# The feed-forward part runs on inside the attention's programs: normalisation in the last phases, last tile in two parts, weights split in the first

## The reference, cut to what matters

```python
x = _layernorm(x + _L0_attn_ref(x, ...), axis=-1)
x = _layernorm(x + _L0_xattn_ref(x, ctx_1024, ...), axis=-1)
x = _layernorm(x + _L0_ffn_ref(x, ...), axis=-1)
...
# _L0_xattn_ref
q = rmsnorm(q, gq)
k = rmsnorm(k, gk)
scores = jnp.einsum('bqhd,bkhd->bhqk', q, k) * scale
attn = jax.nn.softmax(scores, axis=-1)
out = jnp.einsum('bhqk,bkhd->bqhd', attn, v)
return out @ Wo
...
# _L0_ffn_ref
h = jax.nn.gelu(jnp.einsum('lne,he->lnh', x, proj1) + proj1_bias, approximate=False)
out = jnp.einsum('lnh,eh->lne', h, proj2) + proj2_bias
```

## Time and profile before

| | |
|---|---|
| runs | 1362.12 us median, 1360.58 to 1363.41 |
| the profiled execution | 1365.66 us, of it the span 1363.8 us |
| TensorE, busy | 1321.3 us (97%), mean granted clock 0.984 |
| DVE, ACT, POOL, busy | 1104.1 us (81%), 1026.5 us (75%), 1040.8 us (76%) |
| DMA | 45.59 MB, 33 GB/s over the span |
| phase -1 (first key projections) | about 166 to 202 us |
| phase 16 | about 1259 to 1296 us |
| last block | 1296.5 us to the end |

### The profile page before, as it was taken

One profiled execution on the slowest core, in us unless ns is written; L12 is line 12 of the kernel. 1 busy time (PEld: TensorE's weight loads), 2 busy tenths in 40 slices (PEclk: granted clock), 3 DMA queues, 4 the chain that ended last, 5 costly groups with the idle time before them and its releaser, 6 DMA issues. The chain is left out here.

```text
span 1363.8 us, 25118 instructions
## 1 busy us (share of the span) xinstructions
PE 1321.3 (97%) x6366; PEld 1041.6 (76%) x6366; DVE 1104.1 (81%) x1742; ACT 1026.5 (75%) x3157; POOL 1040.8 (76%) x926
## 2 busy tenths in 40 slices
PE   8889899999999999999999999999999999999878
PEld 4667578777777777777777777777777777778667
DVE  5766589888888888888888888888888888875275
ACT  2557688888888888888888888888888888843342
POOL 3733212898989898989898989898989898998840
PEclk9799999999999999999999999999999999999979
DMA  7040000101010101010100000000000010010200
GB/s 246 32 166 1 25 1 9 38 12 35 13 35 13 36 12 34 12 35 12 34 15 32 16 30 19 29 20 26 24 23 27 19 31 16 18 68 25 71 0 28
DMA packets 28012, 45.59 MB, mean 33 GB/s; under 512 B 2720, under 2 KB 23840, under 8 KB 27120
## 3 DMA queue, kind: packets, MB, share of 16 engines
q1 hardware_dynamic: 27168, 44.25, 9.9%
q10 hardware_dynamic: 720, 0.10, 0.0%
HBM read 40.41 MB, written 3.93 MB: 33 GB/s over the span
## 5 line engine op out<-in xcount | busy, mean ns | idle before, releaser
L1302 PE MATMUL xa_k_ps<-wk_parts,xa_ctxT_hi 128*125 128x512 f32 x768 | 377.1, 491 | 6.1 <-DVE wk_parts L1295 5.0
L1245 DVE TENSOR_REDUCE xa_ss<-xa_sq 125x6 f32<-125x768 f32 x360 | 339.4, 943 | 1.0 <-ACT xa_sq L1183 1.0
L1233 DVE TENSOR_TENSOR xa_scores<-xa_s_ps,xa_rk 125x448 f32<-125x448 f32 x384 | 238.5, 621 | 99.8 <-PE xa_s_ps L1304 98.0
L1303 PE MATMUL xa_k_ps<-wk_parts,xa_ctxT_hi 128*125 128x512 f32 x768 | 304.1, 396 | 0.0
L1304 PE MATMUL xa_k_ps<-wk_parts,ctxT_lo 128*125 128x512 f32 x768 | 303.1, 395 | 0.0
L1095 POOL TENSOR_TENSOR xa_den<-probs,xa_den 125x896 f32<-125x896 f32 x128 | 272.2, 2126 | 0.0
L1168 ACT ACTIVATE probs<-xa_scores 125x896 f32<-125x896 f32 x192 | 183.6, 956 | 105.2 <-POOL xa_scores L1084 39.3
L1148 ACT ACTIVATE xa_sq<-xa_k_ps 125x512 f32<-125x512 f32 x360 | 212.2, 589 | 42.3 <-PE xa_k_ps L1304 21.8
L1182 ACT ACTIVATE xa_k_ps<-xa_k_ps 125x128 f32<-125x128 f32 x720 | 189.2, 263 | 30.7 <-PE xa_k_ps L1304 28.6
L1387 PE MATMUL xa_o_ps<-probs,xa_ctx_nat 125*128 125x448 f32 x448 | 205.4, 539 | 0.0
L1084 POOL TENSOR_TENSOR xa_scores<-xa_scores,xa_gmax 125x896 f32<-125x896 f32 x96 | 203.9, 2124 | 0.1
(11 more groups left out here) (186 smaller groups left out, 2364.7 us busy)
## 6 DMA issues: line engine op xcount, KB each, us to landing
xa_ctx_nat<-in_ctx SPq DMA_DIRECT2D x16, 750.0 KB
ctxT_in<-in_ctxT SPq DMA_DIRECT2D x84, 125.0 KB, 2.1
qo<-in_xq_w SPq DMA_DIRECT2D x1, 2048.0 KB, 11.0
qo<-in_xo_w SPq DMA_DIRECT2D x1, 2048.0 KB, 19.0
vo_scratch<-qo SPq DMA_DIRECT2D x2, 1024.0 KB, 5.0
vo<-vo_scratch SPq DMA_DIRECT2D x1, 2048.0 KB, 9.2
ctxT_in<-in_ctxT SPq DMA_DIRECT2D x2, 750.0 KB, 8.9
xq_wkT<-in_xk_wT SPq DMA_DIRECT2D x4, 256.0 KB, 4.3
```

The source lines that it names most:

```text
L1233: dve.tensor_tensor(scores[0:KP, j, :, :], raw, key_scale, ALU.mult).then_inc(s_taken, 1)
L1245: dve.tensor_reduce(ss[:, i // 2, UH * (i % 2):UH * (i % 2) + vector_heads(of)], squares(of, i).rearrange("p (g d) -> p g d", d=XD), AX.X, ...
L1302: pe.matmul(out, l_hi, r_hi, start=first, stop=False)
L1303: pe.matmul(out, l_hi, r_lo, start=False, stop=False)
```

## The change

The separate last block goes; a class `OutputAndMlp` holds its tensors, semaphores and the pieces that the engines' programs of the cross-attention call, with a tail for each engine behind phase 16. There is no barrier between them.

- *Weights.* SP loads the raw weights at the beginning of the block (`load_raw`), into the space of the scores, which phase -1 does not use. POOL splits them in phase -1, a quarter of a weight at steps 1, 3 to 15 (`split_weights`: a cast, a subtraction), SP stores the four parts in DRAM (`store_parts`), DVE waits for all stores before its first score, and SP loads the finished parts in phase 16 (`load_first`, `load_w2`). ACT's and POOL's splits at the end are gone.
- *Residual and normalisation.* The first six tiles of x1 are loaded in phase 15 straight into `z`. The statistics of a tile stand on DVE at steps 16 and 18 of phase 15 and 4, 5, 18 and 18 of phase 16 (`EARLY_STATS`), the variances of tiles 0 to 3 at step 5, ACT's table at step 6, DVE's normalisation at step 9.
- *Subtractions of the last half.* All six are on DVE, at steps 2, 3 and 4 of phase 16 (`LAST_SHIFTS`), and TensorE waits for all of them before the first value product of that half.
- *Denominators.* `TD_LAST` is 6: those of the last half are closed at step 18, not 20.
- *Tile 6.* The first eight heads follow the last phase at once, then the turns of tiles 0 to 3, then the other eight. Its sum and statistics come behind DVE's split of tiles 0 to 3.
- The PSUM banks of the turns, the up- and the down-projections are numbered anew (`TURN_BANKS`, `UP_BANKS`, `DOWN_BANKS`).

```diff
-TD_LAST = 8
+TD_LAST = 6
+LAST_SHIFTS = {2: (-12, -10), 3: (-8, -6), 4: (-4, -2)}
+EARLY_STATS = (B - 1, 16, 0), (B - 1, 18, 1), (B, 4, 2), (B, 5, 3), (B, 18, 4), (B, 18, 5)
...
@@ block.sync
                 if ph.b == B - 1:
...
+                    sp.wait_ge(summed, STEPS * B)
+                    mlp.load_x1(sp)
                 if ph.b == B:
                     sp.wait_ge(s_done, pos_s(Phase(B - 1), STEPS - 1) + 1)
...
+                    sp.wait_ge(max_turned, 2 * B)
+                    mlp.load_first(sp)
+                    sp.wait_ge(exp_done, STEPS * (B - 1) + 18)
+                    sp.wait_ge(p_hi_ready, SPLIT_PAIRS * (2 * B - 1) + 2)
+                    mlp.load_w2(sp)
+                if ph.b == -1:
+                    mlp.store_parts(sp)
 
             sp.dma_start(ident_in, a.ident).then_inc(ident_loaded, 16)
+            mlp.load_raw(sp)
             each_phase(sp, body, 12)
+            mlp.sync_tail(sp)
@@ block.gpsimd
+                    if ph.b == -1 and j % 2 and j < 17:
+                        mlp.split_weights(pool, j // 2)
...
-                    if y is not None and not vector_shifts(y):
+                    if y is not None and not vector_shifts(y) and not (ph.b == B and y >= -KT):
@@ block.scalar
+                    if ph.b == B and j == 6:
+                        mlp.table(act, 0, 0, 1)
@@ block.vector
+                    if ph.b == 0 and j == 0:
+                        dve.wait_ge(mlp.whi_stored[0], 16)
+                        dve.wait_ge(mlp.whi_stored[1], 16)
+                        dve.wait_ge(mlp.wlo_stored, 32)
...
+                    pairs = [y] if y is not None and vector_shifts(y) else []
+                    if ph.b == B:
+                        pairs = list(LAST_SHIFTS.get(j, ()))
+                    for y in pairs:
...
+                    for b, step, tile in EARLY_STATS:
+                        if ph.b == b and j == step:
+                            mlp.early_stats(dve, link, tile)
+                    if ph.b == B and j == 5:
+                        mlp.variances(dve, 0, 0, 1)
+                    if ph.b == B and j == 9:
+                        mlp.normalise(dve, link, 0, 0, 1)
@@ block.tensor
-                            pe.wait_ge(shift_done, ph.at(STEPS, y + KT // 2))
+                            pe.wait_ge(shift_done, ph.at(STEPS, y + (KT if ph.b == B else KT // 2)))
@@ OutputAndMlp (new)
+    def store_parts(self, sp):
+        for i in range(2):
+            sp.wait_ge(self.whi_made, 4 * (i + 1))
+            sp.dma_start(self.a.w_parts[2 * i], self.whi[:, :].bitcast(F32)).then_inc(self.whi_stored[i], 16)
+            sp.wait_ge(self.wlo_made, 4 * (i + 1))
+            sp.dma_start(self.a.w_parts[2 * i + 1], self.wlo[i][:, :].bitcast(F32)).then_inc(self.wlo_stored, 16)
+    def split_weights(self, pool, m):
+        i, c = divmod(m, 4)
+        part = slice(512 * c, 512 * (c + 1))
+        if c == 0:
+            pool.wait_ge(self.wraw_loaded[i], 16)
+            if i:
+                pool.wait_ge(self.whi_stored[0], 16)
+        pool.tensor_copy(self.whi[:, part], self.wraw[i][:, part]).then_inc(self.whi_made, 1)
+        pool.wait_ge(self.whi_made, m + 1)
+        pool.tensor_tensor(self.wlo[i][:, part], self.wraw[i][:, part], self.whi[:, part].bitcast(F32), ALU.subtract
+                           ).then_inc(self.wlo_made, 1)
...
+        pe.wait_ge(o_taken, 2 * B - 1)
+        project_last(0, UH)
+        pe.wait_ge(self.ident_loaded, 16)
+        for n in range(4):
+            turn(n)
+        pe.wait_ge(o_taken, 2 * B)
+        project_last(UH, XH).then_inc(self.z_mm, 1)
+        pe.wait_ge(self.w1_loaded, 32)
+        up(0)
+        up(1)
+        pe.wait_ge(self.w2_loaded, 32)
```

More of the change, by code:

```diff
@@ new lines, in sync_tail, with gpsimd_tail @@
+    def sync_tail(self, sp):
+        for n in range(NT):
+            sp.wait_ge(self.out_ready, n + 1)
+            sp.dma_start(self.a.out[n * P:(n + 1) * P, :], self.z[:, n, :]).then_inc(self.stored, 16)
+        sp.wait_ge(self.stored, 16 * NT)
+    def gpsimd_tail(self, pool, pv_done):
+        pool.wait_ge(pv_done, STEPS * B)
+        pool.wait_ge(self.b_loaded, 32)
+        for n in range(NT):
+            pool.wait_ge(self.x2_ready, n + 1)
+            pool.tensor_tensor(self.xb[:, n, :], self.z[:, n, :], self.b2[:, :], ALU.add).then_inc(self.xb_ready, 1)
@@ new lines, in scalar_tail @@
+    def scalar_tail(self, act):
+        FC, NHB, h_in = self.FC, self.NHB, self.h_in
+        for n in range(0, 4):
+            self.x2T_high(act, n)
+        self.table(act, 0, 1, 2)
+        act.wait_ge(self.b_loaded, 32)
+        for m in range(2 * FC):
+            n, f = divmod(m, FC)
+            if m == self.TURN_BEFORE:
+                for tile in range(4, NT):
+                    self.x2T_high(act, tile)
+            act.wait_ge(self.h_mm, m + 1)
+            if m >= NHB:
+                act.wait_ge(self.h_lo_ready, m - NHB + 1)
+            act.activation(h_in[:, m % NHB, :], self.ps[:, self.UP_BANKS[m % 4], 0:UW], ACT.Gelu,
+                           bias=self.b1[:, f:f + 1]).then_inc(self.h_ready, 1)
+            if m % 2:
+                continue
+            act.wait_ge(self.h_ready, m + 1)
+            act.activation(self.hT_hi[:, f, n * UW:(n + 1) * UW], h_in[:, m % NHB, :], ACT.Copy
+                           ).then_inc(self.h_hi_ready, 1)
+        act.preload_act_table_set(TABLES)
+        for g in range(3):
+            self.table(act, 1, g, 3 + g)
@@ new lines, in stats, with early_stats @@
+    def stats(self, dve, link, i, n, sums, other):
+        z = self.z
+        link(dve.tensor_tensor(z[:, n, :], sums, other[:, n, :], ALU.add))
+        link(dve.bn_stats(self.stat[:, n, :], z[:, n, :]))
+        dve.bn_aggr(self.mv[:, n, :], self.stat[:, n, :]).then_inc(self.stat_ready, 1)
+    def early_stats(self, dve, link, n):
+        dve.wait_ge(self.z_mm, n + 1 if n == EARLY else n // 2 * 2 + 2)
+        if n in (0, EARLY):
+            dve.wait_ge(self.x1_last_loaded if n else self.x1_loaded, 16)
+        self.stats(dve, link, 0, n, self.early_bank(n), self.z)
@@ new lines, in variances, with normalise @@
+    def variances(self, dve, i, g, count):
+        tiles = slice(*self.GROUPS[i][g])
+        dve.wait_ge(self.stat_ready, NT * i + tiles.stop)
+        dve.tensor_scalar(self.lna[:, i, tiles], self.mv[:, tiles, 1], LN_EPS, None, ALU.add).then_inc(self.ln_a, 1)
+    def normalise(self, dve, link, i, g, count):
+        tiles, z, lny = slice(*self.GROUPS[i][g]), self.z, self.lny
+        dve.wait_ge(self.ln_a, count)
+        dve.wait_ge(self.ln_y, count)
+        link(rsqrt_refine(dve, link, lny[:, i, tiles], self.lna[:, i, tiles], self.lnt[:, i, tiles]))
+        for n in range(*self.GROUPS[i][g]):
+            dve.tensor_scalar(z[:, n, :], z[:, n, :], self.mv[:, n, 0:1], lny[:, i, n:n + 1],
+                              ALU.subtract, ALU.mult).then_inc(self.out_ready if i else self.x2_ready, 1)
```

426 lines of the change are left out of this document (188 added, 238 removed).

## The result

The changed kernel takes **1345.16 us**, the median of 4 runs (1344.18 to 1345.90), against 1362.76 for the kernel before beside it: a ratio of 0.9875, 95% interval 0.9861 to 0.9889, so 17.6 us less. The prediction was 1345.3, in a range of 1342 to 1351. Another set of runs on another chip gave 1344.42 and 0.9873 (0.9855 to 0.9892). The profiled execution took 1344.18 us, its span is 1342.4.

What follows compares the result with a forecast made beforehand. TensorE was taken to bound the kernel, losing time in the passage from attention to feed-forward: 17.8 us gained there less 1.0 in the first phase, 16.8 from 1362.12, gives 1345.3 us; range 1342 to 1351.

Steps and rivals of the forecast that it cites:

- What bounds the kernel: TensorE, busy 97% of the span, loses time to waits and a lower clock between attention and feed-forward part.
- Step 1, the last phase: Phase 16: POOL 0.4 us late with its last low part; the last value products end at 1292.0.
- Steps 2 and 3: Tile 6 in halves of 3.44 us around eight turns of 0.88: first up-projection at 1299.85 instead of 1314.85.
- Steps 4 and 5: First 18 up-projection matmuls take 3.64 us, not 6.71; tile 6's turn waits 0.3; the row of 1321.56 moves to 1303.8.
- neither that work nor the normalisation behind it is changed: After the turns of tiles 4 to 6, TensorE's remaining work and the final normalisation keep their length.
- The first phase: Phase -1: POOL's weight splits and the stores cost 1.0 us, range 0 to 4.
- Sum: Whole kernel: 17.8 us gained less 1.0 us lost makes 16.8; from the median 1362.12 that gives 1345.3 us.
- Rival: DVE and POOL block each other: Phase 16: DVE's SBUF instructions wait for POOL's, up to 14.6 us more; 2 to 4 us lost, 1348.5; chance 0.18.
- Rival: the first phase stalls: Phase -1: slow casts or 7 us stores make TensorE and DVE wait 2 us each; 1348.5 to 1350; chance 0.17.
- Slower by the stores: Phase -1: stores of 15 us instead of 5.0 cancel the gain; at 17 us the time is 1366; chance 0.03.
- Part of it without effect: Tile 6 or ACT's table load holds the up-projection, the clock falls, 3.07 us return: 1348.3; chance 0.05.

Runs made afterwards that it cites:

- Experiment 1: Kernel before the change, without POOL's two subtractions splitting the feed-forward weights (ACT makes plain rounded copies instead): 1353.94 us against 1364.19, ratio 0.9921.
- Experiment 6: Changed kernel with POOL's casts of weight parts 4 to 7 in phase -1 each made three times: 1351.09 us, ratio 0.9922 to the kernel before.
- experiment 5: Changed kernel with the last half's denominators closed at step 20 again (`TD_LAST` 8): 1344.16 us, ratio 0.9862 to the kernel before.
- experiment 4: Changed kernel with the last half's subtractions as before, three on DVE and three on POOL: 1346.34 us, ratio 0.9865 to the kernel before.
- experiment 3: Changed kernel with tile 6 projected in one piece ahead of the turns: 1349.70 us, ratio 0.9899 to the kernel before.
- experiment 2: Changed kernel with statistics of tiles 0 to 5 and normalisation of tiles 0 to 3 put back behind phase 16: 1353.21 us, ratio 0.9916.
- experiment 7: Changed kernel with the identity's load and conversion moved behind the first loads of the context: 1343.47 us, ratio 0.9853 to the kernel before.
- number 9: Changed kernel rerun (1344.42 us) beside a second kernel, also with identity later and tile 6's statistics before scaling tiles 4 and 5 (1343.07 us).

## Why the prediction came out right, point by point

- *What bounds the kernel.* Right. Experiment 1 takes the two POOL subtractions away and gets 8.3 of the passage's 19.1 us, by the wait and the clock as read. It is the only part of the 17.8 us that was taken from the old kernel alone; the 3.5 us of the block's end have no run of their own.
- *Step 1, the last phase.* Right in its course. On DVE's subtractions as a common clock the exponential of pair -8 was to end at 1272.7 and ends at 1272.6. Mis-sized was the end: "I take POOL 0.4 us late", where POOL is 1.1 us early; DVE took 0.5 us from it and not 2.2. Hence -0.8 instead of -0.2 in the table.
- *Steps 2 and 3.* Right. Half of tile 6 and the eight turns take 3.46 and 0.87 us for 3.44 and 0.88, the cover of DVE's closing has 2.3 us to spare (1291.02 against 1293.34; 2.1 were written), and the stretch to the first up-projection shrank by 15.1 for 14.8 us.
- *Steps 4 and 5.* The pace of 0.202 us held for 17 of the 18 matmuls, with a clock of 1.00; the second started 0.39 us behind the first. The turns of tile 6 start 0.3 us later than those of tiles 4 and 5 alone would let them (0.16 of it idle), as expected. The stretch shrank by 2.37 us, not 2.76: 0.2 is that first matmul, and 0.16 came from taking 1321.56 out of the chain where TensorE's timeline has the turns start at 1321.40.
- *"neither that work nor the normalisation behind it is changed".* Wrong by 0.85 us. The down-projections alone give 0.54 of it (see the last section); the other 0.3 wasn't traced.
- *The first phase.* The term of 1.0 us was mis-sized: -0.3 in one profile, 0.0 (41.37 against 41.33) in the other. Its two slacks, 1.6 and 0.7 us, were too small. Part 4 started 1.8 us sooner than written (the first high half was whole 0.9 sooner, its store came back after 4.7 us instead of 5.0, and "about 184" rounds 183.4 up) and a part takes 1.9 instead of 2.0, so POOL was about 2 us ahead of the schedule that I wrote. Experiment 6 shows that the place was right: with more work there TensorE stops exactly at step 20.
- *Sum.* 16.8 predicted; 17.6 and 18.2 by medians, 18.9 by the profiles. That the forecast fell within 0.2 us of the median is luck. By the profiles the steps together missed 2.1 us, most of it the first phase (1.3), the end (0.9) and step 1 (0.7), all toward more gain, with 0.7 the other way in the rest; the medians of whole runs gained only 17.6, and the sum was set against a median of 1362.12 where the kernel beside had 1362.76.
- *Rival: DVE and POOL block each other.* The mechanism is there, in full: six of nine instructions, 10.3 us instead of 2.2. The prediction also named a normalisation of over 10 us in phase 16 as a sign of being wrong, and it came, without the loss of time that it was to show. It was to end between 1281 and 1295.5 and ended at 1288.6 on the clock of before (1286.27 on its own), 6.2 us before TensorE wanted the tiles; DVE then stood idle for 0.82 us ahead of the next tile's sum, and POOL lost 0.5 us, not 2. The Trainium skill (SBUF — State Buffer, two separate sides) names two-operand instructions in SBUF as well as the two-port modes: by that rule L53 and L52 can be blocked. L53 was, 1.96 us for its 0.16. L52 took 0.15 us, with POOL's sum starting in the same row time, 1276.00; the same section of the Trainium skill gives the ports to whichever instruction starts first, and the rows can't tell which did.
- *Rival: the first phase stalls.* It doesn't; POOL is 2.6 us ahead. *Slower by the stores:* the stores took 4.2 to 5.9 us in the median, far from 15. *Part of it without effect:* true of `TD_LAST` (experiment 5), whose place I had in the sum only as cover.

What each part is worth, taken alone from the finished change, by the passage in the profiles (and by the medians): early statistics 8.1 us (8.0), tile 6 in halves 5.8 (4.5), DVE's subtractions 2.6 (1.2, not clear of the scatter), `TD_LAST` nothing. These need not add up to the gain, since they share covers. Each keeps TensorE from stopping. The stops of 5.77 and 1.90 us were paid twice, once as a wait and once at the lower clock; the one of 1.72 us (experiment 4) was paid once.

## What to carry to other kernels

A passage between two parts is best priced as three things: the wait, the clock behind it, and what made the awaited engine slow; here two POOL instructions of 4.5 us, neither of them awaited by TensorE, cost eight to ten. DVE's instructions on SBUF alone beside a busy POOL mostly ended with POOL's (six of nine here, 10.3 us for 2.2 of work), so such work belongs where nearly five times its price is covered, as in phase 16 here, or where POOL is idle. And a schedule that fits with 0.7 us of slack on paper deserves an experiment that loads it until it breaks: here the slack was 2.6 us.

## What the runs showed that was not expected

- *Small pauses can cost clock, but length alone doesn't decide it.* A pause of 1.90 us in TensorE's work (experiment 3) was followed by 5 us at a mean of 0.66. In experiment 2 the window that holds most of the 5.77 us pause has 0.67, the one behind it 0.65. But 1.72 us (experiment 4), 2.95 us (experiment 6) and the 0.16 us of the changed kernel left the clock at 1.00. What decides it stays open, so a pause of two or three microseconds should be priced with and without the clock.
- *The slow start of the cross-attention isn't of constant length.* Behind the pause at the block's start the first key matmuls run at half pace, and the moment at which they speed up differs between runs. In experiment 7 the rows show the lower pace from 163.09 to about 168.8, in number 9's second kernel from 161.18 to about 163.9, in the changed kernel to 167.15. TensorE's timelines of these two, the last slow ones and the first fast one:

```profile
163.09 0.76 PE L1331 MATMUL xa_k_ps<-wk_parts,xa_ctxT_hi 128*125 128x512 f32 x1 [3.17 <-DVE wk_parts L1323]
...
168.34 0.63 PE L1331 MATMUL xa_k_ps<-wk_parts,xa_ctxT_hi 128*125 128x512 f32 x1
168.76 0.50 PE L1332 MATMUL xa_k_ps<-wk_parts,xa_ctxT_hi 128*125 128x512 f32 x1
169.10 0.39 PE L1333 MATMUL xa_k_ps<-wk_parts,ctxT_lo 128*125 128x512 f32 x1
```

```profile
161.18 0.76 PE L1331 MATMUL xa_k_ps<-wk_parts,xa_ctxT_hi 128*125 128x512 f32 x1 [3.18 <-DVE wk_parts L1323]
...
163.45 0.63 PE L1333 MATMUL xa_k_ps<-wk_parts,ctxT_lo 128*125 128x512 f32 x1
163.88 0.52 PE L1331 MATMUL xa_k_ps<-wk_parts,xa_ctxT_hi 128*125 128x512 f32 x1
164.24 0.39 PE L1332 MATMUL xa_k_ps<-wk_parts,xa_ctxT_hi 128*125 128x512 f32 x1
```

  A stretch of 5.7 us at half pace costs 1.5 us more than one of 2.7, nearly what experiment 7 can gain. Below 2 us the profiles of such kernels have to be compared stretch by stretch.
- *The same matmuls, another pace at the same clock.* The 168 instructions of the down-projections lie 0.1167 us apart before and in experiment 1, 0.1133 after and in both runs of number 9, and 0.1178 in experiment 3, with a granted clock of 1.00 in the windows of all of these kernels. Over 168 it makes 0.54 us and 0.73. Experiment 3 changes nothing in them but where the program has them. The cause was not looked for and stays open.
